# A table lookup by one-hot matmuls: ScalarE's copy of a field's ids comes by a repeating transfer to SBUF instead of a second matmul into PSUM

## The reference

```
e = stack([tbl_f[ids[:, f]] for f in range(26)], axis=1)
c = concatenate([e, r_dense_x[:, None, :]], axis=1)
z = einsum('bfd,bgd->bfg', c, c)[:, triu_i, triu_j]
h = concatenate([z, r_dense_x], axis=1)
h = maximum(h @ W_top1 + b_top1, 0)
h = maximum(h @ W_top2 + b_top2, 0)
y = h @ W_top3
```

## Time and profile before

| | us |
|---|---|
| median of 3 runs | 119.99 |
| lowest and highest | 119.89, 122.87 |
| the profiled execution | 119.19 |
| its span in the profile | 117.1 |

### The profile page before, as it was taken

How to read it: one execution, slowest core, us unless ns; L and a number is a source line. 1 busy time by engine, 2 the same in 40 slices (tenths; PEclk the granted TensorE clock), 3 DMA queues, 4 the chain that set the end, 5 groups by cost and what they waited for, 6 DMA issues and landing times.

```text
span 117.1 us, 2109 instructions
## 1 busy us (share of the span) xinstructions
PE 108.9 (93%) x720; PEld 88.8 (76%) x720; DVE 78.5 (67%) x159; ACT 75.9 (65%) x173; POOL 72.3 (62%) x76
## 2 busy tenths in 40 slices
PE   5899999989999999998996999999999659999992
PEld 1236668546575588788994999999999559999992
DVE  6599899979999999855576366843568503568121
ACT  5499299999999999956546256651566321556420
POOL 3778877787887877767767777777777730000000
PEclk9999999999999999999999999999999999999999
DMA  4943479937547361112212222113112110000000
GB/s 47 362 141 98 161 241 388 346 104 221 108 167 217 56 225 45 45 45 60 60 45 62 50 50 63 49 45 71 46 45 66 46 45 6 0 0 0 0 6 1
DMA packets 5180, 11.22 MB, mean 96 GB/s; under 512 B 2026, under 2 KB 2538, under 8 KB 5171
## 3 DMA queue, kind: packets, MB, share of 16 engines
q1 hardware_dynamic: 2976, 6.61, 18.0%
q0 software_dynamic: 2176, 4.46, 14.2%
q10 hardware_dynamic: 18, 0.02, 0.1%
HBM read 11.09 MB, written 0.00 MB: 95 GB/s over the span
## 4 chain that ended last, share of the span: by engine, by line
POOL 59%; issue 18%; PE 15%; DMA 4%; DVE 2%; POOLq 1%; ACT 0%; DVEq 0%
POOL rows L262 59%; PE gram_ps L570 6%; DMA rows<-table,ids_sb 2%; PE act_ps L603 2%; PE dve_ps L603 2%; DMA ids_sb<-ids 2%; PE tr_ps L603 1%; POOLq L91 1%; DVE pairs L452 1%; PE top_ps L638 1%; PE dve_ps L625 1%; PE act_ps L625 1%; PE tr_ps L553 1%; PE gram_ps L590 0%; PE tr_ps L582 0%
## 5 line engine op out<-in xcount | busy, mean ns | idle before, releaser
L262 POOL DMA_INDIRECT rows<-table,ids_sb x68 | 71.4, 1050 | 21.9 <-issue 20.4
L570 PE MATMUL gram_ps<-xt 128*122 128x104 f32 x256 | 28.1, 269 | 0.3 <-issue 0.3
L570 PEld LDWEIGHTS gram_ps<-xt 128*122 128x122 f32 x256 | 27.6, 187 | 0.6 <-issue 0.5
L444 DVE COPY gram_sb<-gram_ps 26x104 f32<-26x104 f32 x64 | 17.2, 268 | 10.9 <-PE gram_ps L570 10.5
L290 ACT ACTIVATE gram_sb<-gram_ps 26x104 f32<-26x104 f32 x64 | 15.8, 247 | 11.6 <-PE gram_ps L570 11.2
L537 PE MATMUL gram_ps<-onehot,high 128*128 128x512 f32 x72 | 20.6, 432 | 0.5 <-issue 0.5
L537 PE MATMUL gram_ps<-onehot,low 128*128 128x512 f32 x72 | 18.9, 404 | 0.0
L537 PEld LDWEIGHTS gram_ps<-onehot,high 128*128 128x128 f32 x72 | 13.6, 203 | 5.9 <-issue 1.7
L537 PEld LDWEIGHTS gram_ps<-onehot,low 128*128 128x128 f32 x72 | 12.9, 188 | 5.5 <-issue 3.1
L426 DVE TENSOR_TENSOR onehot<-dve_ps,row_f 128x1024 fp32r<-128x1024 f32 (+1 forms) x10 | 14.4, 1483 | 1.5 <-PE act_ps L514 1.2
L412 DVE COPY xt<-tr_ps 128x512 f32<-128x512 f32 (+3 forms) x12 | 7.2, 604 | 10.0 <-PE tr_ps L553 10.0
(11 more groups left out here) (72 smaller groups left out, 104.0 us busy)
## 6 DMA issues: line engine op xcount, KB each, us to landing
table<-table SPq DMA_DIRECT2D x9, 512.0 KB, 4.0
rows<-table,ids_sb POOLq DMA_INDIRECT x68, 2.6
w1p_sb<-w_pairs SPq DMA_DIRECT2D x1, 768.0 KB
w_sb<-w SPq DMA_DIRECT2D x1, 512.0 KB
dense_sb<-dense SPq DMA_DIRECT2D x1, 256.0 KB, 5.0
w1d_sb<-w_dense SPq DMA_DIRECT2D x1, 256.0 KB
ids_sb<-ids SPq DMA_DIRECT2D x1, 52.0 KB, 1.9
field_ids<-ids_by_field ACTq DMA_DIRECT2D x1, 18.0 KB
```

The lines of the kernel that those rows point to most:

```text
L262: pool.indirect_dma_start(rows[:, t, s - 1, :], None, tables[f], bass.IndirectOffsetOnAxis(ids_sb[:, t, f:f + 1], 0)).then_inc(gathered[t] ...
L444: last = dve.tensor_copy(gram_block(s, q), gram_block_ps(s, q))
L570: last = pe.matmul(gram_ps[s % GRAM_BANKS][0:(Q - 1) * PAD + NJ, k * Q * NJ:(k + 1) * Q * NJ], weights, group[:, :, 1:N_SLOTS], start=True ...
```

## The change

ScalarE's ids no longer come from PE. SP issues, right behind each table, a transfer that reads the field's 512 ids (2 KB of integers) once for every partition and writes them to a new SBUF tensor `ids_wide`, 256 KB, one of two buffers. Each buffer has a semaphore. From the third field on the transfer waits until ScalarE has made `distance` of the field two before, which read the same buffer. ScalarE's `distance` reads `ids_wide` (integers in SBUF) in place of PSUM, and waits for that transfer in place of `ids_spread`. PE's `spread` is one matmul, and `ids_spread` rises after it.

```diff
+        ids_wide = sb("ids_wide", [P, 2, B], I32)
...
-        ids_ps_act = [act_ps[:], top_ps[:].rearrange("p c n -> p (c n)")]
...
+        ids_wide_in = [sem(f"ids_wide_in{i}") for i in range(2)]
...
                 sp.dma_start(table[0:OH_K, o % TABLES], tables[f].rearrange("(p c) d -> p c d", c=OH_CHUNKS)
                              ).then_inc(table_in[o % TABLES], 16)
+                if o >= 2:
+                    sp.wait_ge(distance_ready, o - 1)
+                sp.dma_start(ids_wide[:, o % 2, :], ids_by_field[o:o + 1, :].to_broadcast([P, B])
+                             ).then_inc(ids_wide_in[o % 2], 16)
...
-                act.wait_ge(ids_spread, o + 1)
+                act.wait_ge(ids_wide_in[o % 2], 16 * (o // 2 + 1))
...
-                    last = act.activation(distance[0:OH_K, at:at + B - cols], ids_ps_act[o % 2][0:OH_K, cols:], ACT.Abs,
+                    last = act.activation(distance[0:OH_K, at:at + B - cols], ids_wide[0:OH_K, o % 2, cols:], ACT.Abs,
                                           bias=row_neg[0:OH_K, c:c + 1])
...
-                for ps in (ids_ps_dve[o % 2], ids_ps_act[o % 2]):
-                    last = pe.matmul(ps[0:OH_K], select[:, o, :], field_ids16[:], start=True, stop=True)
-                last.then_inc(ids_spread, 1)
+                pe.matmul(ids_ps_dve[o % 2][0:OH_K], select[:, o, :], field_ids16[:], start=True, stop=True
+                          ).then_inc(ids_spread, 1)
```

## The result

| | us |
|---|---|
| changed kernel, median of 4 runs | 122.38 (121.43 to 123.03) |
| kernel before, median of 4 runs beside it | 119.94 |
| ratio of the compared runs | 1.020, 95% interval 1.013 to 1.027 |
| the changed kernel's profiled execution, its span | 123.03, 121.1 |

The forecast was 120.1 with 118.8 to 122.0 around it. The measured change is +2.0%, and the time lies outside. The changed kernel is slower; whether by more or by less than 2% the interval does not say.

What follows compares the result with a forecast made beforehand. GpSimd's gathers were taken to bound the kernel to 95 us, then TensorE's tail. Gathers 1.3 us later by the tie to `low`, 1.25 earlier by one let through: 119.99 + 0.1 = 120.1 us, range 118.8 to 122.0.

Steps and rivals of the forecast that it cites:

- the reserve: TensorE's single 2.6 us wait for gathered rows before the tail; lateness up to that size would be covered.
- (1): Nine spreads removed from TensorE, 0.26 us each, 2.4 in all; worth nothing on the path.
- (2): ScalarE's `distance` reads SBUF: 0.12 to 0.13 us more per field, main loop's end 0.9 later, within 0 and 4.2.
- (3): Repeating 256 KB transfer behind each table takes 0.65 us of SP's queue; ids late once, 0.3 us in the sum.
- (4): Start: field 0's ids land about 5.8, first pick 0.5 us later, 0.1 to 0.2 left after the first field.
- (5): VectorE's first comparison starts some 0.4 us earlier after one spread; worth nothing, since `low` waits for `high`.
- The sum: TensorE's one-hot work 1.3 us later, within its reserve; last gathers 1.3 later minus 1.25, so 0.1 in all.
- The tie to `low`: GpSimd gathers starting under VectorE's `low` are held until it ends; delays pass on, but near 1.25 us one gather gets through.
- that case: Rival: two gathers let through, -1.2 us, 118.8, TensorE's reserve just covering it; chance 0.12.
- The slower one: Rival: slow repeating transfer, 2.6 us each, ids bound the loop at period 5.3; +3.5, 123.5 us; chance 0.13.
- TensorE stays at half pace longer: Rival: at the start eight matmuls at the lower clock cost 1.7 us more; 121.0 us; chance 0.07.
- the signs named for a wrong forecast: ScalarE gaps ended by `ids_wide` in several fields; no wait for rows at end; period 4.4 or less; first pick after 9.

Runs made afterwards that it cites:

- laid-out ids: Changed kernel with each field's ids laid out 128 times in HBM, not read from one 2 KB line: 118.83 us, ratio 0.992.
- the quiet queue: Kernel before, with repeating transfer, dense vectors and a table appended behind its output, three rounds, each waited for; repeating read 3.0 to 3.4 us, its total time says nothing.
- the filled version: Changed kernel with ids laid out and ahead of tables, weights last, 8 warm-ups, plus 17 zero matmuls in the last tile's wait: 119.74 us, 122.02 without the 17.
- the two versions that came early: Changed kernel with ids ahead of tables, 119.49 us; and that with ids laid out, weights last and 8 warm-up matmuls, 122.02 us.
- The filled version of it: Kernel before with ten matmuls on zeros in TensorE's wait for the last tile's fourth bank of rows: 120.34 us, 119.89 without.

## Why the prediction was wrong

**What bounds the kernel, the reserve.** Right. The reserve of 2.6 us was real and was used as said: TensorE left the loop 5.0 later, the end came 2.2 later at the last copy.

**(1) The removed spreads: nothing.** Right; the run with the spreads put back is not slower.

**(2) ScalarE reads SBUF: 0.12 to 0.13 per field.** Right: `distance` is 0.13 longer (1.65 against 1.52) and the period 4.69 where 4.7 was forecast. Over the loop it comes to 0.7 us with only the first two transfers left, where 0.9 was forecast.

**(3) The repeating transfer.** This is the step that failed most: 0.3 us for the loop, where the runs show 2.8. The gap between a table and its ids was near enough, 0.6 to 1.0 us in seven of the nine fields where 0.65 was forecast, though for field 0 it was 2.0 and for field 3 2.7. What was put at nothing is the delay that the ids bring to all that is in flight behind and beside them. The field that decides is field 4, whose table and ids stand behind the ids of field 3 and 1.5 MB of weights: its table landed 7.9 after issue, where I had taken the median of 4.0, and its ids 8.0 after theirs, 1.9 after ScalarE wanted them. In the kernel before, the table at this place landed in 4.7; laid-out ids bring it to 6.8, the weights behind the last table to 3.8. The rate was too good as well: by the quiet queue's count the repeating read takes 1.3 to 1.7 us of the queue, and the 1.3 that was in the working as the other end was the better one. The argument for 0.65 and against the rival, that tables move in packets of 2 KB too, does not hold: the trace with the quiet queue counts 128 packets for the 512 KB of a table, so 4 KB each. The worst table that I priced was the one issued at 30.0, not the one behind the weights.

**(4) The start.** The step was right in kind and too small. The ids of field 0 landed at 7.0, not 5.8, so the first pick began 1.9 late, not 0.5, and the pick of field 1 1.5 late, where 0.1 was forecast. The same rate is behind part of it, as the run with laid-out ids shows (6.3), and the place in the queue behind the rest: with the ids ahead of the table they landed at 5.3.

**(5) VectorE's earlier start: nothing.** Right; `low` waited 2.0 for `high` at field 0.

**The sum.** In place of 1.3 TensorE was 5.0 late. The profiled executions divide it at the pick of `high` of field 1:

| version | field 1 begins | first dot product | between |
|---|---|---|---|
| kernel before | 14.28 | 53.14 | 38.86 |
| changed kernel | 15.78 | 58.14 | 42.36 |
| only the transfers of fields 0 and 1 | 16.62 | 56.18 | 39.56 |
| weights behind the last table | 16.63 | 56.33 | 39.70 |
| ids ahead of tables, weights last | 15.39 | 54.94 | 39.55 |
| ids laid out | 14.71 | 55.54 | 40.83 |

So 1.5 of the 5.0 arise at the start, 0.7 are ScalarE's reads of SBUF, and 2.8 are late ids in the loop with what follows from them; moving the weights alone takes 2.7 away. Each row is one execution, and how long half pace lasts at the start differs between them.

**The gathers.** The tie to `low` was right, and not only one gather was let through: the last gather was issued at 91.3 instead of 93.8, two paces of 1.25 earlier. It was worth nothing, since TensorE had become the bound. The forecast for that case, "TensorE then becomes the bound", was made for a lateness of 1.3.

**The rivals.** The slower one came nearest, with a chance of 0.13 and a price of 123.5, but not by its own mechanism: it had the ids late in every field, a period of 5.3. The runs show it at the start, at field 4, and for 0.35 at field 7; that the time fell near its price is in part luck. "TensorE stays at half pace longer", 0.07, is not what happened: the first eight picks took 3.69 against 3.78, and the dip behind the hole at field 4 cost some 0.35 us. Of the signs named for a wrong forecast, two came: no wait for rows at the end, and a first pick later than 9.

## What to carry to other kernels

Price a new transfer where it is queued, not at the median: walk the queue for each of its issues, look for the one behind the largest transfer, and price also what it does to the transfers behind it. A copy that an idle engine makes for nothing (nine matmuls of 0.26 us on an engine with 2.6 us of reserve) is not worth replacing by one on a shared queue. And an engine whose clock can fall behind a wait can lose by being early: coming sooner to a wait that ends at a fixed time makes the wait longer, and the work behind it may then run at half pace. Look for a long wait just ahead of a tail that this engine bounds. Where another engine sets the pace, as in the loop here, the same fall costs little.

## What the runs showed of the hardware

**Reading one line 128 times is slow.** On a quiet queue 256 KB read from one 2 KB line landed 3.0 to 3.4 us after issue, 256 KB from distinct lines 2.6 to 2.7; beside other traffic the DMA engines were 0.87 to 0.99 busy at 133 to 187 GB/s. A table queued behind the weights landed 4.7 us after issue without such reads, 7.9 with them, and 6.8 with the same bytes read from distinct lines.

**The clock can fall behind a wait.** After TensorE's idle 2.9 (to 9.9) in the changed kernel its clock stood at 1.2 GHz until 13.3; the spread just ahead of that hole had taken 0.39 us, as at full pace. With ids ahead of tables the hole there was 1.1, and the picks behind it ran at full pace (2.18). After the idle 2.3 (to 32.7) it ran on at full clock for a microsecond and then at 1.2 GHz from 33.8 to 37.2; after 3.84 ahead of the tail it stood there for six, with 29 matmuls where the filled version had 56. After the 2.6 of the kernel before's profile it did not fall. The Trainium skill (TensorE: Matmul & The Clock Gate, HAM oscillation) tells of waits for a transfer after which the matmuls run at the lower clock; the trace agrees, and shows that here a hole of 2.3 us was followed by such a fall too. At a program's start the records do not show it all: the kernel before ran its first eight picks at half pace, 3.78 us, with no hole ahead of them and a recorded clock of 1.00.

**The granted clock tells two times of the kernel before apart.** Over 86 executions beside the experiments, 48 had a mean granted clock of 0.99 or more and lay between 118.75 and 120.10, median 119.3; 38 had less, with a median of 121.6. That the clock falls in the wait ahead of the tail was shown in the profile for the two versions that came early and is inferred for this one, whose own low executions were not profiled. The filled version of it had 1 of 10. A mean under 0.99 is not slow by itself: with only the transfers of fields 0 and 1, four executions at 0.982 to 0.985 took 118.54 to 119.14 us, and four at 1.00 took 119.50 to 120.46.

**VectorE's `low` holds GpSimd's gathers.** In all the versions the gathers longer than 1.2 us, the program's first apart, are those that begin under `low` or up to 0.3 us ahead of it, and each ends 0.80 to 0.83 after `low` ends. Without any change to GpSimd's program the last gather began between 91.3 and 94.8, by how `low` met them.
